# Conditioned norms' scale and shift on two row groups of TensorE; node rows stored in parts of 112 and 13, an edge layer's rows and weights issued behind its first slots

## What is computed

```python
def _L1_gnn_ref(x, edge_index, edge_attr, We, be, eps, W1, b1, W2, b2, gamma, beta, Wf, bf):
    h = x
    for l in range(L):                                  # L = 3
        e = relu(h[src] + edge_attr @ We[l] + be[l])
        agg = segment_sum(e, dst, num_segments=n)
        g = (1.0 + eps[l]) * h + agg
        g = relu(relu(g @ W1[l] + b1[l]) @ W2[l] + b2[l])
        h = (g - mu) * rsqrt(var + LN_EPS) * gamma[l] + beta[l]
    return h @ Wf + bf
```

```python
def _cond_layer_norm(x, cond, sw, sb, bw, bb):
    scale = cond @ sw + sb
    bias = cond @ bw + bb
    return (x - mu) * rsqrt(var + EPS) * (1.0 + scale) + bias
cond = silu(emb @ f_w1 + f_b1) @ f_w2 + f_b2
for i in range(4):
    x = x + attention(_cond_layer_norm(x, cond, s1..., b1...))
    x = x + mlp(_cond_layer_norm(x, cond, s2..., b2...))
```

## Time and profile before

| | us |
|---|---|
| median of three runs | 2763.17 |
| the profiled execution, its own time | 2755.71 |
| its span in the profile | 2753.9 |
| TensorE matmul busy | 2547.8 (93%) |
| VectorE / ScalarE / GpSimd busy | 1170.4 / 756.7 / 726.5 |
| mean granted TensorE clock, share of full speed | 0.957 |

### The profile page before, as it was taken

How to read it: one execution, slowest core, us unless ns; L and a number is a source line. 1 busy time by engine, 2 the same in 40 slices (tenths; PEclk the granted TensorE clock), 3 DMA queues, 4 the chain that set the end, 5 groups by cost and what they waited for, 6 DMA issues and landing times. The chain is left out here.

```text
span 2753.9 us, 33974 instructions
## 1 busy us (share of the span) xinstructions
PE 2547.8 (93%) x11318; PEld 1689.3 (61%) x11318; DVE 1170.4 (42%) x2661; ACT 756.7 (27%) x1487; POOL 726.5 (26%) x717
## 2 busy tenths in 40 slices
PE   4798869989989998899999999999999999789997
PEld 3465437757757655475665766766666666457774
DVE  9713955535535555353343442635222222530001
ACT  0522333323423322153251441521211121111121
POOL 0541955425425400001001010112344443101110
PEclk9898979999989998899999999999999999889998
DMA  3111045435335330110201100102999875548885
GB/s 83 43 55 61 12 136 156 117 123 154 110 122 150 114 128 12 42 46 28 78 1 52 54 21 31 47 19 80 309 288 284 236 220 166 112 160 313 316 288 175
DMA packets 91466, 340.21 MB, mean 124 GB/s; under 512 B 28528, under 2 KB 28656, under 8 KB 83114
## 3 DMA queue, kind: packets, MB, share of 16 engines
q1 hardware_dynamic: 50855, 245.90, 27.7%
q0 software_dynamic: 40448, 92.15, 11.6%
HBM read 338.59 MB, written 36.52 MB: 136 GB/s over the span
## 5 line engine op out<-in xcount | busy, mean ns | idle before, releaser
L84 PE MATMUL ps<-W,HT 128*128 128x320 f32 (+3 forms) x1432 | 533.6, 513 | 2.4 <-ACT HT L2450 1.5
L84 PEld LDWEIGHTS ps<-W,HT 128*128 128x128 f32 (+2 forms) x1432 | 256.5, 190 | 166.3 <-issue 115.2
L84 PE MATMUL ps<-XT,W 128*128 128x250 f32 (+1 forms) x1184 | 326.4, 431 | 2.8 <-ACT XT L1250 1.6
L84 PEld LDWEIGHTS ps<-XT,W 128*128 128x128 f32 x1184 | 225.3, 192 | 100.5 <-issue 17.5
L1028 PE MATMUL ps<-XN,W 128*128 128x512 f32 x504 | 263.6, 606 | 4.2 <-ACT GT L1302 3.5
L1627 POOL TENSOR_TENSOR H<-H,RB 125x512 f32<-125x512 f32 x40 | 50.7, 1267 | 749.8 <-DVE XN L1956 749.8
L2305 POOL DMA_INDIRECT result_rows<-KT,LOGC x110 | 112.6, 1024 | 460.2 <-DVE KT L2484 221.0
L84 PEld LDWEIGHTS ps<-HT,W 128*128 128x128 f32 x1152 | 133.8, 195 | 9.3 <-issue 8.1
L1004 POOL DMA_INDIRECT QT<-node_rows,LOGC x84 | 79.7, 949 | 210.3 <-DMA node_rows<-V 149.9
L1138 PEld LDWEIGHTS ps<-P,QT 128*128 128x128 f32 x672 | 91.0, 197 | 71.5 <-issue 71.5
L84 PE MATMUL ps<-HT,W 128*128 128x128 f32 x1152 | 134.1, 278 | 0.8 <-DVE HT L2902 0.8
(11 more groups left out here) (570 smaller groups left out, 4276.4 us busy)
## 6 DMA issues: line engine op xcount, KB each, us to landing
W<-in_L_ffn_w SPq DMA_DIRECT2D x38, 2048.0 KB, 7.4
W<-in_L_ffn_Wgu SPq DMA_DIRECT2D x92, 640.0 KB
W<-in_L_ffn_Wd SPq DMA_DIRECT2D x92, 320.0 KB
W<-in_L_gnn_Wqkv SPq DMA_DIRECT2D x4, 3072.0 KB, 10.1
W<-in_L_gnn_W SPq DMA_DIRECT2D x5, 2048.0 KB, 24.4
W<-in_L_gnn_Wm SPq DMA_DIRECT2D x4, 2048.0 KB, 7.9
W<-result_rows SPq DMA_DIRECT2D x5, 1344.0 KB
RB<-in_L_gnn_rows SPq DMA_DIRECT2D x24, 256.0 KB, 3.5
```

Source lines behind the costliest of these rows:

```text
L84: last = nc.tensor.matmul(out, lhs(k), rhs(k), start=(k == 0), stop=(k == nk - 1))
```

## The change

1. `cond` gives scale and shift each a group of 32 rows: the weights of the shift move to partitions 32 to 48 of affine, GT holds cond twice (rows 0 to 16 and 32 to 48), and each matmul takes 32 rows with its tile position. The loads of 17 x 1024 become two of 17 x 512. The 64-column f_w2 and a 64-row f_b2 with the ones in it make both copies of GT at once, and GpSimd's copy of ones (line 998) goes.
2. Each store of node rows becomes two DMAs, 112 and 13 rows.
3. SP waits for the relu of slot 11 of the layer before it issues rows and W1 with W2.
4. In layers 0 and 1 the new H of tile t - 1 (`finished`) is written after tile t's first scalar_tensor_tensor; the next V (`stored_rows`) stays where it was.
5. Eight unused index buffers go.

```diff
@@ SP, edge layers
             for layer in range(NL):
                 for t in range(T):
                     sp.wait_ge(s["hb_ready"], T * layer + t + 1)
-                    sp.dma_start(hb[t * R:(t + 1) * R, :], b.V[0:R, t, :]).then_inc(s["hb_stored"], 16)
+                    for lo, hi in PARTS:
+                        sp.dma_start(hb[t * R + lo:t * R + hi, :], b.V[lo:hi, t, :]).then_inc(s["hb_stored"], 16)
+                sp.wait_ge(s["relu_ready"], NSLOT * layer + GR)
                 if layer == 0:
@@ GpSimd
-            nc.gpsimd.tensor_copy(b.GT[0:32, :], b.ident[0:32, 16:17].to_broadcast([32, NP])).then_inc(s["ones"], 1)
             for layer in range(NL):
-                pool.wait_ge(s["hb_stored"], 16 * T * (layer + 1))
+                pool.wait_ge(s["hb_stored"], 32 * T * (layer + 1))
@@ VectorE, edge layers
-                        finished(layer, t - 1)
+                        stored_rows(layer, t - 1)
+                        if layer == NL - 1:
+                            finished(layer, t - 1)
...
                     c.mark(v.scalar_tensor_tensor(b.H[0:R, t, :], b.V[0:R, t, :], b.mv[0:R, t, 0:1], GAMMA[0:R, :],
                                                   ALU.subtract, ALU.mult))
+                    if t and layer < NL - 1:
+                        finished(layer, t - 1)
+                stored_rows(layer, T - 1)
                 finished(layer, T - 1)
@@ ScalarE
-                    act.wait_ge(s["ones"], 1)
-                    nc.scalar.activation(halves(b.GT[0:16, :]), b.slot(1)[0:16, :, 0:HF], ACT.Identity,
-                                         bias=b.cols[0:16, C["f_b2"]:C["f_b2"] + 1]).then_inc(s["cond"], 1)
+                    nc.scalar.activation(halves(b.GT[0:64, :]), b.slot(1)[0:64, :, 0:HF], ACT.Identity,
+                                         bias=b.cols[0:64, C["f_b2"]:C["f_b2"] + 1]).then_inc(s["cond"], 1)
@@ SP, transformer (the same for affine[1])
-                sp.dma_start(b.affine[0][0:17, :], sb[:, 0:1024]).then_inc(p.g2_affine[0], 16)
+                sp.dma_start(b.affine[0][0:17, 0:512], sb[:, 0:512]).then_inc(p.g2_affine[0], 16)
+                sp.dma_start(b.affine[0][32:49, 512:1024], sb[:, 512:1024]).then_inc(p.g2_affine[0], 16)
@@ TensorE, cond
-                    last = nc.tensor.matmul(b.ps[0:R, 6 + a, :], b.GT[:, t * R:(t + 1) * R],
-                                            b.affine[n][:, a * D:(a + 1) * D], start=True, stop=True)
+                    last = nc.tensor.matmul(b.ps[0:R, 6 + a, :], b.GT[32 * a:32 * a + 32, t * R:(t + 1) * R],
+                                            b.affine[n][32 * a:32 * a + 32, a * D:(a + 1) * D], start=True, stop=True,
+                                            tile_position=(32 * a, 0))
```

More of the change, by code:

```diff
@@ L876, in l1_gnn_block @@
                    "next_row", "t_mm", "t_out", "wf_mm", "x_biased", "x_added", "vec_in", "angles", "embedded", "h1_mm", "h1", "cond_mm", "cond",
-                   "ones", "gate_in", "scale_in", "w1_in", "w2_in", "xvar", "xstd", "hvar", "hstd", "xn_ready", "hn_ready",
+                   "gate_in", "scale_in", "w1_in", "w2_in", "xvar", "xstd", "hvar", "hstd", "xn_ready", "hn_ready",
                    "tx_mm", "tx_out", "th_mm", "th_out", "logits", "copied", "shifted", "exp_ready", "e_mm", "e_out", "y_mm",
@@ L982, in _ @@
                 sp.wait_ge(s["affine_zero"], n + 1)
-                sp.dma_start(b.affine[n][0:17, :], A["L2_gnn_sb"][0, :, 1024 * n:1024 * (n + 1)])\
-                    .then_inc(p.g2_affine[n], 16)
+                for part in range(2):
+                    at = 1024 * n + 512 * part
+                    sp.dma_start(b.affine[n][32 * part:32 * part + 17, 512 * part:512 * part + 512],
+                                 A["L2_gnn_sb"][0, :, at:at + 512]).then_inc(p.g2_affine[n], 16)
             sp.dma_start(b.W[:, 6144:8192], A["L2_gnn_wo"][0]).then_inc(p.g2_wo, 16)
@@ L1063, in final, with embed @@
                     .then_inc(s["wf_mm"], 1)
-            def embed(w, rhs, done):
-                matmul_columns(nc, b.slot(1), 16, lambda k: w, lambda k: rhs, 1).then_inc(s[done], 1)
+            def embed(w, rhs, m, done):
+                matmul_columns(nc, b.slot(1), m, lambda k: w, lambda k: rhs, 1).then_inc(s[done], 1)
             def normed_turned(t):
@@ L1157, in _ @@
                     pe.wait_ge(s["embedded"], 2)
-                    embed(b.emb_w[0:NF, 0:16], emb, "h1_mm")
+                    embed(b.emb_w[0:NF, 0:16], emb, 16, "h1_mm")
                 second(layer, 3)
@@ L1165, in _ @@
                     pe.wait_ge(s["h1"], 1)
[L1166 removed]
+                    embed(b.emb_w[0:16, 16:80], emb_hidden, 64, "cond_mm")
                     pe.wait_ge(s["cond"], 1)
@@ L1345, in _, with stored_rows @@
             c = Chain(dve, s["chain"])
-            def finished(layer, t):
+            def stored_rows(layer, t):
                 dve.wait_ge(s["std"], 1 + T * layer + t + 1)
@@ L1353, in finished @@
                                            ALU.add).then_inc(s["hb_ready"], 1)
+            def finished(layer, t):
+                if layer < NL - 1:
                     dve.wait_ge(s["hb_ready"], T * (layer + 1) + t + 1)
@@ L1609, in _ @@
                 sp.wait_ge(s["cond_mm"], norm(layer, 1, T - 1))
-                sp.dma_start(b.affine[1][0:17, :], sb[:, 1024:2048]).then_inc(p.g2_affine[1], 16)
+                sp.dma_start(b.affine[1][0:17, 0:512], sb[:, 1024:1536]).then_inc(p.g2_affine[1], 16)
+                sp.dma_start(b.affine[1][32:49, 512:1024], sb[:, 1536:2048]).then_inc(p.g2_affine[1], 16)
                 sp.wait_ge(s["mb2_added"], T * (layer + 1))
@@ L1826, in plus_one @@
             def plus_one(layer, n):
-                act.wait_ge(p.g2_affine[n], 16 * (layer + 1))
+                act.wait_ge(p.g2_affine[n], 32 * (layer + 1))
                 nc.scalar.activation(b.affine[n][0:32, 0:D], b.affine[n][0:32, 0:D], ACT.Identity,
@@ L3006, in build @@
         b.smax, b.nmax, b.den = sb("smax", [128, 20]), sb("nmax", [128, 20]), sb("den", [128, 20])
-        b.scatter_idx = [sb(f"scatter_idx{u}", [128, 1], I32) for u in range(SLOT_UNROLL)]
-        b.gather_idx = [sb(f"gather_idx{u}", [128, 1], I32) for u in range(SLOT_UNROLL)]
         qt, kt = (x[:, :, :].rearrange("p k n -> p (k n)") for x in (b.QT, b.KT))
@@ L3075, in pad, with twice @@
         return out
+    def twice(x, next_row):
+        out = np.zeros(64, f)
+        for at in (0, 32):
+            out[at:at + 16], out[at + 16] = x, next_row
+        return out
     freq = pad(np.tile(np.arange(1, 33, dtype=f) * f(TWO_PI / 16), 2))
     cols = [col(a["L0_gnn_b1"]), col(a["L0_gnn_g1"]), col(a["L0_gnn_be1"]), col(a["L0_gnn_b2"]), col(a["L0_gnn_g2"]),
-            col(a["L0_gnn_be2"]), a["L0_ffn_b1"].T, freq, pad(a["L2_gnn_f_b1"]), pad(a["L2_gnn_f_b2"])]
+            col(a["L0_gnn_be2"]), a["L0_ffn_b1"].T, freq, pad(a["L2_gnn_f_b1"]),
+            pad(twice(a["L2_gnn_f_b2"], f(1)))]
     out = {
@@ L3098, in _layout @@
         "L1_ffn_w2": np.concatenate(list(a["L1_ffn_w2"]), axis=1),
-        "L2_gnn_f_w1": a["L2_gnn_f_w1"], "L2_gnn_f_w2": a["L2_gnn_f_w2"],
+        "L2_gnn_f_w1": a["L2_gnn_f_w1"], "L2_gnn_f_w2": np.stack([twice(x, f(0)) for x in a["L2_gnn_f_w2"]]),
         "L2_gnn_sb": np.concatenate([np.concatenate([a[f"L2_gnn_{n}_w"], a[f"L2_gnn_{n}_b"][:, None, :]], axis=1)
```

5 lines of the change are left out of this document (2 added, 3 removed).

## The result

The changed kernel took 2743.43 us, the median of four runs (2740.06 to 2751.77), against 2763.73 for the kernel before beside it (2762.22 to 2764.74). The ratio is 0.9932, 95% interval 0.9909 to 0.9954. The forecast was 2728, a ratio of 0.9873. So it is faster, inside the range, but by 20 us where 35 were forecast. The same file was timed again beside two groups of experiments on other chips: 0.9838 (0.9820 to 0.9856) and 0.9847 (0.9834 to 0.9860), 45 and 43 us. Why the same change is worth 20 us in one place and 44 in another is what the experiments had to find.

The account below looks back on a forecast made before the run. TensorE, busy 93% of the span, was taken to bound the kernel. Edge layers 28 us and norms 7 us, together 35, came off the 2763.2 us median, giving 2728 us; range 2706 to 2750, the forecast's own 2720 to 2736.

Parts of the forecast that it names:

- The edge layers, 28 us: Starts of edge layers: faster stores and earlier first gathers gain 12.7, 8 and 6.9 us; bounds 20 and 33.
- Stores: Layer starts: two-part stores move 256 KB in 1.2 us, not 3.05; last V to first gather 3.6 us, not 5.17.
- Slot 0 right behind the third product: Sign for layers 0 and 2: TensorE starts slot 0 once the third edge product ends, 393.6 us in layer 0.
- Slot 6 was at 620.30 and would be at 600.8 + 6 x 1.75: Layer 1: slots follow every 1.75 us, so slot 6 comes at 611.3, 9.0 us earlier; 8 taken.
- The third: Rival, edge layers: the burst behind slot 11 delays gathers, giving back three times 4.7 us; 2742 us, chance 0.08.
- The norms, 7 us: Conditioned norms on two row groups: 1.54 us a tile against 1.72, 0.18 gained on each of 40 tiles.
- shift 1 stands behind it in program order, and can only run beside scale 2: Conditioned norm's four passes: only one pair overlaps, so three times 0.43 us, 1.29, instead of four.
- the mode's price: Conditioned norms: changing the array between 128 and 32 rows costs 0.25 us a norm tile; bounds 0.1 and 0.4.
- Rival 1: Conditioned norms: full overlap, 0.61 a tile; with some clock gain it sets the range's bottom, 2706 us; chance 0.2.
- each microsecond of TensorE removed from the transformer moves everything behind it forward: Transformer: TensorE is busy 90.00 of 90.00 us, so its savings shorten the execution; nothing waits for a fixed moment.
- What was costed at nothing: Moved rows and W, VectorE's order, copy of ones, wider f_w2 product and eight new loads: no cost or gain.
- Rival 5: Conditioned norms: 32-row passes are paid in full with their loads, 3.1 us for four passes; chance 0.05.

Follow-up runs that it names:

- the edge part alone: Kernel before plus stores in two parts, rows and W behind slot 11, and VectorE's new order, norms unchanged: 2724.32 us, 0.9889.
- the first group: One chip, kernel before 2754.06 us: norms alone 2739.01, edge part alone 2724.32, changed kernel again 2709.09, changed kernel with six gathers of lead 2724.32.
- the third group: One chip, kernel before 2754.25 us: changed kernel 2711.29; with rows and W in small parts and lead six 2714.75, every gather spaced 2828.31, every fourth 2728.81.
- the norms alone: Kernel before plus the conditioned norms on two row groups; stores, SP's order and VectorE's order as before: 2739.01 us, 0.9944.
- with six: Changed kernel, a gather waiting for the sum of the slot six before its own instead of twelve: 2724.32 us, 0.9885.
- one row group: Changed kernel with scale and shift both on the first row group, rows 0 to 31: 2771.90 us, 1.0037.
- the second group: One chip, kernel before 2761.36 us: changed kernel with one row group 2771.90, gathers spaced 2746.50; kernel before with split stores 2756.26, SP's wait 2764.71.
- the spaced gathers: Changed kernel, gathers 2 to 11 of a layer each waiting until the gather two before has landed: 2746.50 us, 0.9949.

## Why the prediction was right, and where it was wrong

**The edge layers, 28 us.** Right without the stall, and by its own steps: 29.7 us for the edge part alone in the first group. Layer by layer it was 10.2, 9.4 and 9.3 against 12.7, 8 and 6.9. Part of the excess in layer 0 and part of the shortfall in layer 2 come from the trace that the terms were read from, since its slots 0 to 7 are themselves shaped by the stall. Stores: last V to first gather 3.2 us in layer 0 (to be compared to 3.6) and 2.6 in layer 1. First gather to use: 3.5 us (3.4). The DMA engines moved 169 GB/s in a window on layer 1's last store (592.1 to 593.6), where over 150 was forecast. Slot 0 right behind the third product: yes.

In the first result this term gave 3.7 us. The step that failed is "Slot 6 was at 620.30 and would be at 600.8 + 6 x 1.75", and its likes in layers 0 and 2: that slots follow each other at 1.75 us once the first is there. From slot 0 to slot 12 the changed kernel took 31.5, 30.7 and 29.0 us in the first result against 21.0, 22.8 and 21.0 in the third group, 26 us in the three layers. No rival had this. The third came nearest in what it costs, but named W's burst, and placed it behind slot 11.

**What in the profile of before could have told.** The prediction gave the six slots of layer 2 that took 15.2 us to gathers that come late beside 3 MB. VectorE's row in layer 0 of the same trace says "4.70 <-remote", not "<-DMA": a gather was not what it waited for. Passing over a wait whose releaser is unknown was the mistake; the change moved slot 0 away from the burst's end, and the wait became 10.93 us. In the kernel before it cost little: between slots 0 and 12 of layers 0 and 2 it took 25.6 and 25.7 us, against 23.4 and 22.9 in the kernel with the norms alone on a chip without it, and in layer 1 none.

**The norms, 7 us.** Right in sign, too small: 15 us for the norms alone. Two sizes were off. The step "shift 1 stands behind it in program order, and can only run beside scale 2" is wrong. The four start in program order in the profile's rows, but as pairs 7 ns apart, and both passes overlap. The Trainium skill, "TensorE: Matmul & The Clock Gate", Part 3, has a pack's span as one matmul plus some 4 ns for each further tile; the pair's 7 ns are near that. That the next pair follows after 0.52 us and not 0.43 isn't the pairing's doing: with one row group the first and last steps are as long, 0.53 and 0.52. And the mode's price, taken at 0.25 us, is 0.38: 0.1 ahead, 0.1 behind the next instruction's first pass, and the rest in those two longer steps. By these numbers a norm tile gains 0.85 - 0.38 = 0.47 us. Rival 1 (full overlap, 0.61 a tile) had the mechanism, at a chance of 0.2.

Times 40 that is 18.8 us; the trace of the whole transformer shows 13 to 14. Twelve tiles, three in each layer's attention, gain their 0.47 and lose it again at once, since there TensorE then waits for ScalarE:

```profile
PE ps L1722 <- ACT HT L1876: 4.2, 12, 0.4
```

(PE's waits of 1105 to 1850 us in the changed kernel; the kernel with the edge part alone has no such line.) The prediction's "each microsecond of TensorE removed from the transformer moves everything behind it forward" holds for the other 28.

**What was costed at nothing.** W behind slot 11 held up no slot from 12 to 73 of the changed kernel in either group without the stall, so the lead of twelve covers it; with six it doesn't, and slot 16 of each layer waits 4 to 7 us. The wider f_w2 product, the copy of ones and VectorE's order show in no wait; VectorE's order wasn't tried alone.

**Rival 5**, that 32-row passes are paid in full with their loads, is out: with one row group four passes take 1.90 us, where it had 3.1. The chances for the sign were right; the time, 2728, was 15 us too low in the first result and about 9 us too high by the ratios of the other two (0.9873 against 0.984). That the first result lies inside the range is partly luck: the edge layers fell short by 24 us in its profile, and the norms, priced at half of what they gave, took some of it back.

## What stays open

Why some chips show the stall and others don't, with the same program and the same transfers. All six profiles of the first result and the second group have it (one chip or two), the kernel before included; none of the eight on the other two chips has. What in the burst of gathers holds up the news of TensorE's ends isn't shown; that the stall follows the burst rests on the spaced gathers, in one kernel and three layers, beside W's burst, and only there.

The difference between the kernels before (2763.7 and 2761.4 us against 2754.1 and 2754.3) is probably partly this and partly some 4 to 5 us ahead of edge layer 0. Those come from one stretch, from 84 to 101 us, where GpSimd gathers edge attributes one per 1.25 to 1.6 us. It takes 17.1 to 18.3 us in the six profiles and 12.0 to 12.3 in the eight, and ScalarE waits longer for TensorE in it. In the changed kernel of the first result and then of the third group:

```profile
96.65 0.62 ACT L487 ACTIVATE QT<-QT 128x500 bf16<-128x500 f32 x1 [2.42 <-PE ps L315]
102.38 0.62 ACT L487 ACTIVATE QT<-QT 128x500 bf16<-128x500 f32 x1 [3.80 <-PE ps L315]
```

```profile
96.37 0.62 ACT L487 ACTIVATE QT<-QT 128x500 bf16<-128x500 f32 x1 [0.36 <-PE ps L315]
```

The DMA engines are busy 0.18 and 0.19 of that time. So it looks like the same thing with other gathers, far from W and with lightly loaded DMA engines; no experiment touched it.

One rival stands untested: the recording of the trace. In the eight profiles without the stall no semaphore rise is missing for the 6068 or 6069 increments that the engines' instructions make; in the six with it 90 to 125 are. From 390 to 405 us the changed kernel's first profile has 48 rises of all semaphores, and the third group's has 204 in the 15 us from the same pass on; in the transformer both have 2205. So records are lost around the stall, and also later, from 2000 to 2200 us, where no wait is put down to "remote", but none in the transformer. The waits are real in these executions, since VectorE, ScalarE and GpSimd all stand still. But every execution on record comes with a span and a granted clock, so each was recorded, and no run tells whether the stall brings the loss of records, or the recording the stall, or what an execution without a recording would take on these chips.

## What to carry to other kernels

A wait that the profile ascribes to "remote" is a wait of unknown cause; before a change moves work away from or towards it, price it as if it grew. See too whether semaphore rises are missing from the trace around it. Time a change on more than one chip when its gain rests on how quickly engines hear of each other: 20 and 45 us were both measured, with intervals (0.9909 to 0.9954 and 0.9820 to 0.9856) that don't meet. Two small products side by side on two row groups and in two PSUM banks cost little more than one, as long as few of them stand between passes of the full array: the change of mode took back 45% of what the overlap gave. Splitting each product further, over four groups, wasn't tried.

## What was not expected of the hardware

The ends of TensorE's products can reach VectorE and GpSimd 7 to 10 us late, several at once, while GpSimd issues indirect DMAs one per 1.25 us, on some chips and not on others, and records of semaphore rises are missing from the traces in the same stretches. Float32 products on two row groups overlap in both of their passes, starting 7 ns apart. A round trip between 128-row and 32-row passes costs 0.38 us (2.96 against 2.58), about half of it in a first and a last step that are 0.1 us longer each.
